# A mixture-of-experts kernel that stops zeroing its row buffer in stripes and loads rows with direct transfers on GpSimd

## The chip, the cores and the metric

One core of a Trainium2 chip runs the whole kernel as one program. The metric is the device time of a run in microseconds (us). The core has five engines that run side by side and meet only at semaphores: TensorE (PE, with its weight loads shown as PEld), VectorE (DVE), ScalarE (ACT), GpSimd (POOL) and SyncE (SP). Transfers issued by SP, ACT and POOL are carried out by the core's 16 DMA engines.

## The reference

Eight batches of 256 tokens with 128 channels go through three stages. Stage 1 and stage 3 are the same block: RMS norm, attention with rotary embedding, a window and a sink, projection, then a layer of 32 experts of which each token takes four. Stage 2 is another attention. Cut to what matters:

```
x = x + ffn_block(x) / 2          # stage 1: attention, then experts
x = x + mid_attention(layernorm(x))
x = x + ffn_block(x) / 2          # stage 3: same weights as stage 1

ffn_block: h  = x + attention(rmsnorm(x))
           g  = rmsnorm(h);  top4 experts of g @ gate_w + gate_b, softmax weights
           out = h + sum over the 4 of weight * (silu-gated up(g)) @ W_down
```

## The kernel before

The order of the program on each engine is `attention(layers[0])`, `experts(0)`, a barrier, `attention(layers[1])`, a barrier, `attention(layers[2])`, `experts(1)`. So five stretches follow each other: first attention, first experts, middle attention, last attention, last experts. The first and the last attention come from the same Python code and the same plan; they differ only where the code says `L is layers[0]`.

**Attention of a stage with experts.** Work is cut into frames; a frame makes scores of one group of heads for one tile of 128 tokens (PE, line 793), and side work (rotary projections, turning, projection, gate) is put between by a plan made in Python. In a rotary step DVE writes `rot_b` (line 1043, one of `RING` = 4 buffers), POOL adds it into `qT` or `keyT` with rows swapped by two accumulating transfers (`add_swapped`, line 1527), and DVE may write the same buffer of `rot_b` again only when those have landed. At a tile's end the reciprocal row sums make a round trip through DRAM: SP stores them (`turned<-rT`, line 622), loads them back spread over the partitions (`spread<-turned`, line 637), and POOL multiplies (`yT`, line 1628) before PE can project. SP also loads the expert weights during this stretch, in both stages.

**Routing.** After the gate, each tile's rows are scattered by POOL to `routed`, a DRAM buffer with a region of 2048 rows for each expert (`send`, line 1610, four indirect transfers of a tile). The row's place is expert times `REGION` plus the number of earlier rows of this expert.

**Zeroing.** An expert's rows are worked off in blocks of 128, counted from the start of its region, so its last block reads past its rows. All that a block may read must be finite. Therefore, in the first attention only, ACT issues sixteen transfers of 2 MB each (`blank_next`, line 1431), each of which zeroes one stripe of 128 rows in all 32 regions ahead of the tile whose rows could first reach it; POOL waits for a stripe (`blanked`) before it accounts for the tile.

**Experts.** DVE and PE make the plan: number of blocks of each expert, first row of each of the 96 blocks (`block_rows`, and `rows_at` with the partition added), and offset of its weights (`block_w`). Then 24 groups of four blocks are taken: rows are loaded into one of `XSLOTS` = 7 slots, two blocks by SP (line 688, direct, the row read into a register with line 683) and two by POOL (line 1709, indirect, with the rows' indices in `rows_at`); PE turns them (line 921), multiplies (931, 942, 950), and SP stores the answers. Answers are gathered by POOL later.

Of the kernel before, what the change touches and what calls it, by code (L numbers as in the profile page):

```python
# [42 lines left out]
REGION = TOKENS  # L43
# [4 lines left out]
XROWS = E * REGION + P  # L48
# [120 lines left out]
def primed(name):  # L169
# [11 lines left out]
    w_loaded=16 * E, count_full=1, nb_step=3, end_full=1, end_step=2, plan_full=1, plan_step=7,  # L181
# [139 lines left out]
def build(nc, x, table, masks, ffn_w, mid_w, columns, rows, w_up, w_down, out):  # L321
# [6 lines left out]
    with ExitStack() as ctx:  # L328
# [88 lines left out]
        earlier = sb("earlier", [P, E], BF16)  # L417
# [9 lines left out]
        nb_more = sb("nb_more", [E, TILES])  # L427
        nb_one = sb("nb_one", [E, 1])
        nb = sb("nb", [E, P], BF16)
        chosen = sb("chosen", [E, 2, NBLOCKS])  # L430
        block_row = sb("block_row", [P, NBLOCKS])
# [3 lines left out]
        rows_at = sb("rows_at", [P, NBLOCKS], U32)  # L435
# [20 lines left out]
        blanked = [sem(f"blanked{n}") for n in range(4)]  # L456
# [113 lines left out]
        def _(sp):  # L570
# [35 lines left out]
            def attention(L):  # L606

                if L.ffn:
                    if L is layers[0]:
                        sp.dma_start(routed[E * REGION:XROWS, :].rearrange("(p r) d -> p (r d)", p=P),  # L610
                                     nothing[:, 0:D]).then_inc(pads_zero, 16)
                S = L.signals

                def store_rows(k, lt):

                    tile, par = 4 * k + lt, lt % 2
                    turn = 2 * k + lt // 2
# [48 lines left out]
                body()  # L666

            def experts(number):
# [4 lines left out]
                sp.wait_ge(pads_zero, 16)  # L673
                sp.wait_ge(*S.at("plan_step", 7))
# [30 lines left out]
        def _(pe):  # L705
# [3 lines left out]
            def attention(L):  # L709
# [35 lines left out]
                def tail_step(k, misc, use, kind, arg):  # L745
# [21 lines left out]
                    elif kind == "place":  # L767
# [3 lines left out]
                        last = pe.matmul(misc[:, 0:E], mk[:, B_ONE:B_ONE + P], earlier[:, :], start=False, stop=True)  # L771
# [121 lines left out]
            def experts(number):  # L893
# [4 lines left out]
                pe.matmul(ps[0:E, BANK_XT, 0:NBLOCKS], earlier[:, :], mk[:, B_ONE:B_ONE + NBLOCKS],  # L898
# [4 lines left out]
                pe.matmul(ps[:, BANK_XT, 256:256 + E], nb[:, :], mk[0:E, B_BEFORE:B_BEFORE + E],  # L903
                          start=True, stop=True).then_inc(S["end_full"], 1)
                pe.wait_ge(*S.at("end_step", 2))
                pe.matmul(ps[:, BANK_Y, 0:2 * NBLOCKS], ones, chosen[:, :, :].rearrange("e a b -> e (a b)"),
                          start=True, stop=True).then_inc(S["plan_full"], 1)
                pe.wait_ge(*S.at("plan_step", 7))
# [69 lines left out]
        def _(dve):  # L978
# [24 lines left out]
            def attention(L):  # L1003
# [124 lines left out]
                def tail_step(k, misc, use, kind, arg):  # L1128
# [32 lines left out]
                    elif kind == "place":  # L1161
# [11 lines left out]
                        dve.tensor_copy(row_at[:, lt, :], place[:, :]).then_inc(S["place_step"], 1)  # L1173
# [63 lines left out]
            def experts(number):  # L1237
                S = moe[number]
                count = ps[0:E, BANK_XT, 0:NBLOCKS]
# [9 lines left out]
                dve.tensor_reduce(nb_one[:, :], nb_more[:, :], AX.X, ALU.add).then_inc(S["nb_step"], 1)  # L1249
                dve.wait_ge(*S.at("nb_step", 2))  # L1250
                dve.tensor_copy(nb[:, :], nb_one[:, 0:1].broadcast_to([E, P])).then_inc(S["nb_step"], 1)
                dve.wait_ge(*S.at("end_full", 1))
                dve.wait_ge(*S.at("nb_step", 3))
                dve.tensor_tensor(chosen[:, 0, :], block[0:E, :], end, ALU.is_ge).then_inc(S["end_step"], 1)
                dve.wait_ge(*S.at("end_step", 1))
                dve.tensor_tensor(chosen[:, 1, :], chosen[:, 0, :], nb[:, 0:NBLOCKS], ALU.mult)\
                    .then_inc(S["end_step"], 1)
                dve.scalar_tensor_tensor(first_at[:, :], ps[:, BANK_XT, 256:256 + E], float(P),
                                         tb[:, T_BASE:T_BASE + E], ALU.mult, ALU.subtract)\
                    .then_inc(S["plan_step"], 1)  # L1260
                dve.wait_ge(*S.at("plan_full", 1))
                dve.scalar_tensor_tensor(block_row[:, :], block, 0.0, plan[:, 1, :], ALU.add, ALU.subtract)\
# [3 lines left out]
                dve.wait_ge(*S.at("plan_step", 2))  # L1266
                dve.tensor_scalar(block_row[:, :], block_row[:, :], float(P), None, ALU.mult)\
                    .then_inc(S["plan_step"], 1)
                dve.wait_ge(*S.at("plan_step", 4))
                dve.scalar_tensor_tensor(region_row[:, :], plan[:, 0, :], float(REGION), block_row[:, :],  # L1270
                                         ALU.mult, ALU.add).then_inc(S["plan_step"], 1)
                dve.wait_ge(*S.at("plan_step", 5))
                dve.tensor_scalar(block_rows[:, :], region_row[:, :], float(E * REGION), None, ALU.min)\
                    .then_inc(S["plan_step"], 1)
                dve.tensor_scalar(rows_at[:, :], region_row[:, :], float(E * REGION), tb[:, T_PART:T_PART + 1],
                                  ALU.min, ALU.add).then_inc(S["plan_step"], 1)
# [69 lines left out]
        def _(act):  # L1346
# [9 lines left out]
            def attention(L):  # L1356
# [68 lines left out]
                def blank_next(k, lt):  # L1425

                    if k:
                        act.wait_ge(blanked[lt], 16 * k)
                    to = routed[0:E * REGION, :].rearrange("(e t r) d -> t e (r d)", e=E, t=TILES)
                    to = to[4 * k + lt:4 * k + lt + 1].rearrange("o e (c n) -> (o e) c n", n=BLANK)  # L1430
                    act.dma_start(to, nothing[0:E, :].unsqueeze(1).broadcast_to([E, STRIPE // BLANK, BLANK]))\
                        .then_inc(blanked[lt], 16)

                def body():
                    for frame in L.plan:
                        if L is layers[0]:
                            for k, lt in at_slot(frame, (2, 6, 10, 14)):
                                blank_next(k, lt)
# [61 lines left out]
        def _(pool):  # L1500
# [4 lines left out]
            def attention(L):  # L1505
# [89 lines left out]
                def account(k, lt):  # L1595
# [101 lines left out]
            def experts(number):  # L1697
# [72 lines left out]
```

## Time and profile before

| what | value |
|---|---|
| median of 3 runs | 1367.88 us (1364.82 to 1372.32) |
| profiled execution, device time | 1374.12 us |
| its span in the profile | 1372.3 us |
| busy in the span: PE, DVE, POOL, ACT | 1009.0, 806.2, 790.2, 570.7 us |
| mean granted TensorE clock | 0.879 of full speed |
| bytes moved by the transfers | 137.75 MB |
| `routed<-nothing` on ACT's queue | 16 issues of 2048 KB, 13.6 us to landing |

The busy times overlap and say nothing of which stretch waits for what; that has to be read from each stretch. "us to landing" is from the issue of a transfer to the semaphore that says it is in place.

### The profile page before, as it was taken

Reading aid. Unit: us, or ns where it says so; the run is one execution under the profiler, and the core shown is the slowest. Engines: PE = TensorE matmul, PEld = TensorE weight load, DVE = VectorE, ACT = ScalarE, POOL = GpSimd, SP = SyncE. Lnnn points to the kernel's source line nnn. Section 1 sums busy time; section 2 is a strip of 40 time slices with the busy share of each in tenths; the row PEclk is TensorE's granted clock in tenths of the full one; section 3 lists DMA queues with packets and bytes.
Section 4 is the critical chain, followed back from the end, with each engine's and each line's share of the span. In section 5 each row is a group of like instructions: output and inputs, shape, how many; then the busy total and the mean of one; then the engine's idle time right before and its main releaser. Section 6 shows DMA issues by size and latency. Waiting matters only on the chain.

```text
span 1372.3 us, 23277 instructions
## 1 busy us (share of the span) xinstructions
PE 1009.0 (74%) x6906; PEld 710.3 (52%) x6906; DVE 806.2 (59%) x2096; ACT 570.7 (42%) x2204; POOL 790.2 (58%) x1020
## 2 busy tenths in 40 slices
PE   2969788797735893599999947989888884689300
PEld 2646565564524773356666635656556553577200
DVE  4747777775531442378788637888888764143122
ACT  0535454454502441255565622655555461344100
POOL 3325587665577512657775314477877757751476
PEclk9889999998957997599999977999999996799755
DMA  7778999977613432011111103454543321343222
GB/s 181 144 166 178 197 206 202 192 159 163 142 51 102 133 101 62 21 36 32 36 41 32 24 16 62 105 124 90 129 99 84 66 55 49 109 134 99 69 63 59
DMA packets 121814, 137.75 MB, mean 100 GB/s; under 512 B 16864, under 2 KB 96992, under 8 KB 121696
## 3 DMA queue, kind: packets, MB, share of 16 engines
q1 hardware_dynamic: 86928, 57.99, 15.8%
q0 software_dynamic: 24064, 44.07, 15.2%
q10 hardware_dynamic: 10704, 34.21, 12.1%
q8 instruction: 62, 1.02, 0.3%
q14 instruction: 56, 0.46, 0.1%
HBM read 57.24 MB, written 58.07 MB: 84 GB/s over the span
## 4 chain that ended last, share of the span: by engine, by line
PE 38%; DVE 12%; POOL 9%; issue 7%; DMA 2%; ACT 1%; POOLq 1%; DVEq 0%; ACTq 0%
PE ps L931 6%; PE ps L820 5%; POOL shared L1719 4%; PE ps L838 4%; PE ps L950 4%; PE ps L733 3%; PE ps L855 3%; PE ps L793 3%; DVE top L1101 3%; PE ps L759 2%; DVE shift L1104 2%; PE ps L942 2%; PE ps L921 2%; DVE pT L1109 2%; DVE xr L1184 1%
## 5 line engine op out<-in xcount | busy, mean ns | idle before, releaser
L1373 ACT ACTIVATE prob<-ps,shift 128x128 f32<-128x128 f32 (+1 forms) x768 | 312.8, 422 | 165.0 <-DVE shift L1104 162.5
L1101 DVE TENSOR_REDUCE top<-ps 128x4 f32<-128x512 f32 (+1 forms) x192 | 182.7, 952 | 64.7 <-PE ps L793 32.2
L838 PE MATMUL ps<-tb,prob 128*128 128x128 f32 x1152 | 170.5, 285 | 1.5 <-DVE pT L1109 1.0
L1628 POOL TENSOR_TENSOR yT<-yraw,spread 128x1024 f32<-128x1024 f32 (+1 forms) x48 | 82.5, 1720 | 152.3 <-DMA spread<-turned 150.9
L838 PEld LDWEIGHTS ps<-tb,prob 128*128 128x128 f32 x1152 | 130.3, 144 | 70.5 <-issue 60.6
L1373 ACT ACTIVATION_READ_ACCUMULATOR prob<-ps,shift 128x1 f32 x768 | 158.7, 207 | 0.0
L1109 DVE COPY pT<-ps 128x512 f32<-128x512 f32 x192 | 131.4, 684 | 42.4 <-PE ps L838 42.2
L1610 POOL DMA_INDIRECT routed<-row_out,row_at x128 | 132.9, 1038 | 27.1 <-issue 26.6
L855 PE MATMUL ps<-pT,v 128*64 128x256 f32 x768 | 114.7, 405 | 23.3 <-issue 14.9
L1395 ACT ACTIVATE yraw<-ps 128x256 f32<-128x256 f32 x128 | 49.1, 383 | 184.6 <-PE ps L855 152.8
L793 PE MATMUL ps<-keyT,qT 64*128 64x256 f32 (+1 forms) x1024 | 125.5, 366 | 0.0
L1709 POOL DMA_INDIRECT qT<-routed,rows_at x96 | 90.7, 945 | 57.3 <-PE ps L921 29.3
L1527 POOL DMA_DIRECT2D qT<-rot_b x128 | 115.8, 1165 | 5.5 <-DVE qT L1043 5.2
L759 PE MATMUL ps<-wf,yT 128*128 128x128 f32 x512 | 76.0, 311 | 43.2 <-POOL yT L1628 40.7
L820 PE MATMUL ps<-shared,qT 128*128 128x256 f32 (+1 forms) x256 | 107.1, 519 | 0.5 <-ACT prob L1373 0.2
L793 PEld LDWEIGHTS ps<-keyT,qT 64*128 64x128 f32 x1024 | 81.8, 196 | 44.6 <-issue 37.8
L733 PE MATMUL ps<-xT,wf 128*128 128x256 f32 x320 | 93.4, 424 | 11.3 <-DVE pT L1109 5.8
L1291 DVE COPY prob<-ps 128x512 f32<-128x512 f32 x48 | 33.2, 692 | 115.8 <-PE ps L942 110.0
L1043 DVE SCALAR_TENSOR_TENSOR rot_b<-ps,bias_col,tb 128x256 f32<-128x256 f32 x160 | 69.5, 476 | 51.6 <-PE ps L733 30.7
L1719 POOL DMA_INDIRECT shared<-answers,answer_at x64 | 61.3, 957 | 60.2 <-DMA answers<-yraw 41.0
L759 PEld LDWEIGHTS ps<-wf,yT 128*128 128x128 f32 x512 | 71.8, 224 | 46.4 <-issue 44.4
L1634 POOL DMA_INDIRECT swapped<-answers,answer_at x64 | 62.4, 975 | 55.2 <-DMA answers<-yraw 41.4
(156 smaller groups left out, 1902.9 us busy)
## 6 DMA issues: line engine op xcount, KB each, us to landing
routed<-nothing ACTq DMA_DIRECT2D x16, 2048.0 KB, 13.6
qT<-rot_b POOLq DMA_DIRECT2D x128, 128.0 KB, 4.2
spread<-turned SPq DMA_DIRECT2D x64, 256.0 KB, 4.7
answers<-yraw SPq DMA_DIRECT2D x48, 256.0 KB, 2.3
shared<-in_w_up SPq DMA_DIRECT2D x32, 256.0 KB
qT<-routed SPq DMA_DIRECT2D x96, 64.0 KB, 2.0
keyT<-rot_b POOLq DMA_DIRECT2D x32, 128.0 KB, 3.2
shared<-in_w_down SPq DMA_DIRECT2D x32, 128.0 KB
```

The source lines that it names most:

```text
L733: last = pe.matmul(misc[:, n * T:(n + 1) * T], w[:, 0:P], xT[:, :], start=True, stop=True)
L759: last = pe.matmul(misc[:, 0:D], yT[:, n * P:(n + 1) * P], w, start=(n == 0), stop=(n == blocks - 1))
L793: last = pe.matmul(ps[:, bank + side, T * n:T * n + keys(lt)], qT[rows, j, 2 * g + n, q0:q0 + P], keyT[rows, j, g // 2, 0:keys(lt)], start ...
L820: last = pe.matmul(to, q, heads, start=behind, stop=not behind and n == 1)
L838: last = pe.transpose(ps[:, BANK_SIDE + bank, h * P:(h + 1) * P], prob[:, s % 4, h, c * P:(c + 1) * P], ident)
L855: last = pe.matmul(y[DH * side:DH * side + DH, 0:2 * P], v[:, j, c, at:at + DH], pT[:, s % 2, c, 2 * P * side:2 * P * side + 2 * P], start ...
L1101: dve.tensor_reduce(top1[:, s % 2, :], score_view(L, s, lt), AX.X, ALU.max, negate=True)\
L1109: dve.tensor_copy(pT[:, s % 2, 0, :], ps[:, BANK_SIDE + L.turned[k, s][0][0], :]).then_inc(S["pT_ready"], 1)
L1373: last = act.activation(prob[:, s % 4, h, 0:keys(lt)], score_view(L, s, lt)[:, h, :], ACT.Exp, bias=shift[:, lt % 2, one:one + 1], accum_o ...
L1527: pool.dma_start(to[n:P:2].rearrange("p n t -> p (n t)"), rot_b[1 - n:P:2, r % RING, :], accum_op=ALU.add).then_inc(S[f"swapped{r % RING}" ...
L1610: pool.indirect_dma_start(routed, bass.IndirectOffsetOnAxis(row_at[:, lt, n:n + 1], 0), row_out[:, lt, :], None).then_inc(S[f"sent{lt}"], 16)
L1719: pool.indirect_dma_start(last_answers[:, tile, n, :], None, answers, bass.IndirectOffsetOnAxis(answer_at[:, tile, n:n + 1], 0))\
```

## The change

The expert's blocks are counted from the end of its rows: its last block ends with its last row, and its first block may begin ahead of its first row. For that the rows of an expert start 128 rows into its region, and only these 128 rows ahead of each region are zeroed, once, by one SP transfer of 2 MB at the start. The sixteen stripe transfers and the waits for them go. Two more count matmuls, four more DVE instructions and fewer others make the plan. POOL reads the block's first row into a register and issues a direct transfer, as SP does, in place of the indirect one.

```
-REGION = TOKENS
+REGION = TOKENS + 4 * P
-XROWS = E * REGION + P
+XROWS = E * REGION + 2 * P
+NO_ROWS = E * REGION + P
...
-                        sp.dma_start(routed[E * REGION:XROWS, :].rearrange("(p r) d -> p (r d)", p=P),
+                        sp.dma_start(routed[NO_ROWS:XROWS, :].rearrange("(p r) d -> p (r d)", p=P),
                                      nothing[:, 0:D]).then_inc(pads_zero, 16)
+                        ahead = routed[0:E * REGION, :].rearrange("(e r) d -> e (r d)", e=E)[:, 0:STRIPE]
+                        sp.dma_start(ahead.rearrange("e (c n) -> e c n", n=BLANK),
+                                     nothing[0:E, :].unsqueeze(1).broadcast_to([E, STRIPE // BLANK, BLANK]))\
+                            .then_inc(pads_zero, 16)
...
-                dve.tensor_tensor(nb_more[:, :], count[:, 0:TILES], tb[0:E, T_IOTA16:T_IOTA16 + TILES], ALU.is_gt)\
+                dve.tensor_tensor(nb_more[:, :, :], count[:, :, 0:TILES],
+                                  tb[0:E, T_IOTA16:T_IOTA16 + TILES].unsqueeze(1).broadcast_to([E, 2, TILES]), ALU.is_gt)\
                     .then_inc(S["nb_step"], 1)
...
-                def blank_next(k, lt):
-
-                    if k:
-                        act.wait_ge(blanked[lt], 16 * k)
-                    to = routed[0:E * REGION, :].rearrange("(e t r) d -> t e (r d)", e=E, t=TILES)
-                    to = to[4 * k + lt:4 * k + lt + 1].rearrange("o e (c n) -> (o e) c n", n=BLANK)
-                    act.dma_start(to, nothing[0:E, :].unsqueeze(1).broadcast_to([E, STRIPE // BLANK, BLANK]))\
-                        .then_inc(blanked[lt], 16)
...
-                        if L is layers[0]:
-                            for k, lt in at_slot(frame, (2, 6, 10, 14)):
-                                blank_next(k, lt)
...
-                    if L is layers[0]:
-                        pool.wait_ge(blanked[lt], 16 * (k + 1))
-                    pool.tensor_tensor(earlier[:, :], earlier[:, :], picked[:, :], ALU.add).then_inc(S["picked"], 1)
+                    if L is layers[0] and tile == 0:
+                        pool.wait_ge(pads_zero, 32)
+                    pool.tensor_tensor(earlier[:, 0:E], earlier[:, 0:E], picked[:, :], ALU.add).then_inc(S["picked"], 1)
...
-                pool.wait_ge(pads_zero, 16)
-                pool.wait_ge(*S.at("plan_step", 7))
+                pool.wait_ge(pads_zero, 32)
+                pool.wait_ge(*S.at("plan_step", 3))
...
-                        pool.indirect_dma_start(
-                            rows_in[:, g % XSLOTS, b, :], None, routed,
-                            bass.IndirectOffsetOnAxis(rows_at[:, c:c + 1], 0)).then_inc(S[f"x_pooled{g % XSLOTS}"], 16)
+                        at = pool.value_load(block_rows[0:1, c:c + 1], min_val=0, max_val=XROWS - P)
+                        pool.dma_start(rows_in[:, g % XSLOTS, b, :], routed[bass.ds(at, P), :])\
+                            .then_inc(S[f"x_pooled{g % XSLOTS}"], 16)
```

The instruction order on ACT at the start of the first attention, before; `yraw`, `prob` and `sexp` are the attention's, `routed<-nothing` is a stripe of zeros:

```order
L1373 ACTIVATE prob,total<-ps,shift 128x128 x8
L1431 DMA routed<-nothing 32x16x1024
L1395 ACTIVATE yraw<-ps 128x256
L1373 ACTIVATE prob,total<-ps,shift 128x128 x4
L1395 ACTIVATE yraw<-ps 128x256
```

The same place in the changed kernel:

```order
L1388 ACTIVATE prob,total<-ps,shift 128x128 x8
L1410 ACTIVATE yraw<-ps 128x256
L1388 ACTIVATE prob,total<-ps,shift 128x128 x4
L1410 ACTIVATE yraw<-ps 128x256
L1388 ACTIVATE prob,total<-ps,shift 128x128 x4
```

All sixteen such rows are gone from ACT. SP's rows at the end of the initial loads in the changed kernel, where the one transfer of 32x16x1024 numbers now stands right behind the pads and ahead of the first store of row sums:

```order
L610 DMA routed<-nothing 128x128
L613 DMA routed<-nothing 32x16x1024
L626 DMA turned<-rT 16x128
L641 DMA spread<-turned 64x4x256 x2
L655 DMA shared<-in_w_up 128x2x256
```

POOL at the start of the first experts, before: the last rows of the last tile are sent, then 48 indirect loads follow each other.

```order
L1604 TENSOR_TENSOR earlier<-earlier,picked 128x32
L1605 COPY place_of<-place 128x4
L1610 DMA routed<-row_out,row_at 65664x128 x8
L1709 DMA qT<-routed,rows_at 128x128 x48
L1634 DMA swapped<-answers,answer_at 128x128 x8
```

And in the changed kernel, where each of the 48 loads is a register load, three register instructions (ISA) and a transfer:

```order
L1607 TENSOR_TENSOR earlier<-earlier,picked 128x32
L1608 COPY place_of<-place 128x4
L1613 DMA routed<-row_out,row_at 82176x128 x8
L1712 TENSOR_LOAD block_rows
L1712 ISA x2
L1713 ISA
L1713 DMA qT<-routed 128x128
L1712 TENSOR_LOAD block_rows
L1712 ISA x2
L1713 ISA
L1713 DMA qT<-routed 128x128
```

The loads keep their place on POOL; what stands between them is new.

## Rows read from the trace of the kernel before

The columns of the first group are: stretch, its length, busy us and instructions of PE, PEld, DVE, ACT and POOL, granted clock, DMA share, GB/s. A timeline row is: start, us, engine, line, what, and in brackets the idle time before it and what ended that.

**Rows 1.** Windows from first to last score, first and last attention

```profile
38.50:369.30 330.80, 270.92 (x1870) 183.88 (x1871) 228.43 (x602) 161.71 (x697) 196.46 (x281) 0.91 0.84 178
840.60:1128.20 287.60, 259.50 (x1872) 176.84 (x1871) 234.51 (x602) 163.71 (x698) 196.83 (x281) 0.97 0.41 92
```

**Rows 2.** Timeline, POOL: the last tile accounted, first and last attention

```profile
407.00 0.24 POOL L1604 TENSOR_TENSOR earlier<-earlier,picked 128x32 bf16<-128x32 bf16 x1 [1.02 <-DVE row_at L1173]
...
1160.52 0.24 POOL L1604 TENSOR_TENSOR earlier<-earlier,picked 128x32 bf16<-128x32 bf16 x1 [1.03 <-DVE row_at L1173]
```

**Rows 3.** Timeline, SP's queue: first tile's store in both, load back in the first

```profile
64.12 0.33 SPq L622 DMA_DIRECT2D turned<-rT  x1
73.58 3.23 SPq L637 DMA_DIRECT2D spread<-turned  x2
...
866.31 0.32 SPq L622 DMA_DIRECT2D turned<-rT  x1
```

**Rows 4.** Timeline, POOL: the first tile's multiplication, first and last attention

```profile
87.52 2.34 POOL L1628 TENSOR_TENSOR yT<-yraw,spread 128x1024 f32<-128x1024 f32 x1 [26.98 <-DMA spread<-turned]
...
872.70 2.36 POOL L1628 TENSOR_TENSOR yT<-yraw,spread 128x1024 f32<-128x1024 f32 x1 [9.99 <-DMA spread<-turned]
```

**Rows 5.** Waits (us, times, longest), 19 to 408 us, then 797 to 1161

```profile
POOL yT L1628 <- DMA spread<-turned: 112.4, 15, 27.0
...
POOL yT L1628 <- DMA spread<-turned: 38.5, 11, 10.0
```

**Rows 6.** Landing of `turned<-rT` (line 622), 60 to 408, then 860 to 1161

```profile
DMA to landing us min/median/max: 6.7/8.2/9.4
...
DMA to landing us min/median/max: 1.4/1.4/1.7
```

**Rows 7.** DMA queues: ACT's, packets, MB and share of 16 engines, 38 to 369

```profile
q10 hardware_dynamic: 8167, 32.47, 47.7%
```

**Rows 8.** Landing of the swaps (line 1527): at 27, 40 to 52, 220 to 410

```profile
DMA to landing us min/median/max: 3.5/3.6/3.6
...
DMA to landing us min/median/max: 12.1/12.1/12.1
...
DMA to landing us min/median/max: 2.7/7.9/12.2
```

**Rows 9.** Timeline before the first scores; at the end the last attention's rstd alone

```profile
23.61 2.02 POOL L1527 DMA_DIRECT2D keyT<-rot_b  x2 [6.80 <-DVE keyT L1043]
27.88 0.87 DVE L1043 SCALAR_TENSOR_TENSOR rot_b<-ps,bias_col,tb 128x256 f32<-128x256 f32 x2
31.27 2.46 POOL L1557 TENSOR_TENSOR rstd<-powers,minus_half 128x4 f32<-128x4 f32 x1
...
857.28 1.03 POOL L1557 TENSOR_TENSOR rstd<-powers,minus_half 128x4 f32<-128x4 f32 x1 [5.30 <-DVE powers L1020]
```

**Rows 10.** Timeline, start of the first experts

```profile
411.30 0.27 DVE L1275 TENSOR_SCALAR rows_at<-region_row,tb 128x96 uint32<-128x96 f32 x1
419.71 1.00 POOL L1709 DMA_INDIRECT qT<-routed,rows_at  x1 [2.27 <-issue]
420.50 14.34 SPq L688 DMA_DIRECT2D qT<-routed  x14
421.01 0.97 POOL L1709 DMA_INDIRECT qT<-routed,rows_at  x1 [0.30 <-issue]
426.12 1.09 PE L921 MATMUL ps<-tb,qT 128*128 128x128 f32 x4 [1.23 <-DMA qT<-routed,rows_at]
```

**Rows 11.** Lines 683 (SP) and 1527 (POOL): ns min/median/max

```profile
L683 SPq TENSOR_LOAD <-block_rows x96: 261/273/662, 418.9 to 1255.7; - x96
...
L1527 POOL DMA_DIRECT2D qT<-rot_b x128: 848/1178/2030, 25.2 to 1088.9; - x128
```

**Rows 12.** Chain of waits in the first experts, one step of two groups

```profile
485.33 1.73 PE ps L931 x8
...
489.60 1.73 PE ps L931 x8
```

More of the change, by code:

```diff
@@ L416, in build @@
         picked = sb("picked", [P, E], BF16)
-        earlier = sb("earlier", [P, E], BF16)
+        earlier = sb("earlier", [P, E + 1], BF16)
         ranks = sb("ranks", [P, TOPK, E])
@@ L425, in build @@
         answer = swapped[:, :, :].rearrange("p a b -> p (a b)").rearrange("p (s t k d) -> p s t k d", s=2, t=2, k=TOPK)
-        nb_more = sb("nb_more", [E, TILES])
-        nb_one = sb("nb_one", [E, 1])
+        nb_more = sb("nb_more", [E, 2, TILES])
+        nb_two = sb("nb_two", [E, 2])
+        short_by = sb("short_by", [E, 2])
+        step_of = sb("step_of", [E, 2])
         nb = sb("nb", [E, P], BF16)
         chosen = sb("chosen", [E, 2, NBLOCKS])
-        block_row = sb("block_row", [P, NBLOCKS])
         region_row = sb("region_row", [P, NBLOCKS])
@@ L455, in build @@
         tail_step = sem("tail_step")
-        blanked = [sem(f"blanked{n}") for n in range(4)]
         prep = sem("prep")
@@ L672, in experts @@
                     sp.wait_ge(*L.signals.at(f"sent{n}", BATCH * 32))
-                sp.wait_ge(pads_zero, 16)
-                sp.wait_ge(*S.at("plan_step", 7))
+                sp.wait_ge(pads_zero, 32)
+                sp.wait_ge(*S.at("plan_step", 3))
                 def store(g):
@@ L770, in tail_step @@
                         pe.matmul(misc[:, 0:E], mk[:, B_ONE:B_ONE + P], mk[:, B_BASE:B_BASE + E], start=False, stop=False)
-                        last = pe.matmul(misc[:, 0:E], mk[:, B_ONE:B_ONE + P], earlier[:, :], start=False, stop=True)
+                        last = pe.matmul(misc[:, 0:E], mk[:, B_ONE:B_ONE + P], earlier[:, 0:E], start=False, stop=True)
                     last.then_inc(S["misc_full"], 1)
@@ L897, in experts @@
                 pe.wait_ge(*layers[2 * number].signals.at("picked", TILES))
-                pe.matmul(ps[0:E, BANK_XT, 0:NBLOCKS], earlier[:, :], mk[:, B_ONE:B_ONE + NBLOCKS],
+                for n in range(2):
+                    pe.matmul(ps[0:E, BANK_XT, n * NBLOCKS:(n + 1) * NBLOCKS], earlier[:, n:n + E],
+                              mk[:, B_ONE:B_ONE + NBLOCKS], start=True, stop=True)
+                pe.matmul(ps[:, BANK_Y + 1, E:2 * E], mk[:, B_ONE:B_ONE + P], earlier[:, 0:E],
                           start=True, stop=True).then_inc(S["count_full"], 1)
@@ L902, in experts @@
                           start=True, stop=True)
-                pe.matmul(ps[:, BANK_XT, 256:256 + E], nb[:, :], mk[0:E, B_BEFORE:B_BEFORE + E],
+                pe.matmul(ps[:, BANK_Y + 1, 0:E], nb[:, :], mk[0:E, B_UPTO:B_UPTO + E],
                           start=True, stop=True).then_inc(S["end_full"], 1)
-                pe.wait_ge(*S.at("end_step", 2))
+                pe.wait_ge(*S.at("end_step", 3))
                 pe.matmul(ps[:, BANK_Y, 0:2 * NBLOCKS], ones, chosen[:, :, :].rearrange("e a b -> e (a b)"),
                           start=True, stop=True).then_inc(S["plan_full"], 1)
-                pe.wait_ge(*S.at("plan_step", 7))
+                pe.wait_ge(*S.at("plan_step", 5))
                 pe.wait_ge(*S.at("w_loaded", 16 * E))
@@ L1172, in tail_step @@
                             dve.wait_ge(*S.at(f"sent{lt}", 64 * k))
-                        dve.tensor_copy(row_at[:, lt, :], place[:, :]).then_inc(S["place_step"], 1)
+                        dve.tensor_scalar(row_at[:, lt, :], place[:, :], float(P), None, ALU.add).then_inc(S["place_step"], 1)
                 def combine(b, par):
@@ L1238, in experts @@
                 S = moe[number]
-                count = ps[0:E, BANK_XT, 0:NBLOCKS]
+                count = ps[0:E, BANK_XT, 0:2 * NBLOCKS].rearrange("e (n c) -> e n c", n=2)
                 end = ps[0:E, BANK_HT, 0:NBLOCKS]
@@ L1250, in experts @@
                 dve.wait_ge(*S.at("nb_step", 2))
-                dve.tensor_copy(nb[:, :], nb_one[:, 0:1].broadcast_to([E, P])).then_inc(S["nb_step"], 1)
+                dve.tensor_copy(nb[:, :], nb_two[:, 0:1].broadcast_to([E, P])).then_inc(S["nb_step"], 1)
+                dve.scalar_tensor_tensor(short_by[:, :], nb_two[:, :], float(-P),
+                                         count[:, :, 0:1].rearrange("e n c -> e (n c)"), ALU.mult, ALU.add)\
+                    .then_inc(S["nb_step"], 1)
@@ L1252, in experts @@
+                dve.wait_ge(*S.at("nb_step", 4))
+                dve.scalar_tensor_tensor(step_of[:, 0:1], short_by[:, 1:2], float(REGION), short_by[:, 0:1],
+                                         ALU.add, ALU.subtract).then_inc(S["nb_step"], 1)
+                dve.wait_ge(*S.at("nb_step", 5))
+                dve.scalar_tensor_tensor(step_of[:, 1:2], nb_two[:, 0:1], float(-P), step_of[:, 0:1],
+                                         ALU.mult, ALU.add).then_inc(S["nb_step"], 1)
                 dve.wait_ge(*S.at("end_full", 1))
-                dve.wait_ge(*S.at("nb_step", 3))
@@ L1254, in experts @@
                 dve.tensor_tensor(chosen[:, 0, :], block[0:E, :], end, ALU.is_ge).then_inc(S["end_step"], 1)
                 dve.wait_ge(*S.at("end_step", 1))
-                dve.tensor_tensor(chosen[:, 1, :], chosen[:, 0, :], nb[:, 0:NBLOCKS], ALU.mult)\
+                dve.wait_ge(*S.at("nb_step", 6))
+                dve.tensor_scalar(chosen[:, 1, :], chosen[:, 0, :], step_of[:, 1:2], None, ALU.mult)\
                     .then_inc(S["end_step"], 1)
-                dve.scalar_tensor_tensor(first_at[:, :], ps[:, BANK_XT, 256:256 + E], float(P),
-                                         tb[:, T_BASE:T_BASE + E], ALU.mult, ALU.subtract)\
-                    .then_inc(S["plan_step"], 1)
+                dve.wait_ge(*S.at("end_step", 2))
@@ L1261, in experts @@
+                dve.tensor_scalar(chosen[0:1, 1, :], chosen[0:1, 1, :], short_by[0:1, 0:1], float(P), ALU.add, ALU.add)\
+                    .then_inc(S["end_step"], 1)
                 dve.wait_ge(*S.at("plan_full", 1))
-                dve.scalar_tensor_tensor(block_row[:, :], block, 0.0, plan[:, 1, :], ALU.add, ALU.subtract)\
+                dve.scalar_tensor_tensor(region_row[:, :], block, float(P), plan[:, 1, :], ALU.mult, ALU.add)\
                     .then_inc(S["plan_step"], 1)
@@ L1265, in experts @@
                     .then_inc(S["plan_step"], 1)
-                dve.wait_ge(*S.at("plan_step", 2))
-                dve.tensor_scalar(block_row[:, :], block_row[:, :], float(P), None, ALU.mult)\
+                dve.wait_ge(*S.at("plan_step", 1))
+                dve.tensor_scalar(block_rows[:, :], region_row[:, :], float(NO_ROWS), None, ALU.min)\
+                    .then_inc(S["plan_step"], 1)
+                dve.scalar_tensor_tensor(first_at[:, :], ps[:, BANK_Y + 1, 0:E], float(P),
+                                         tb[:, T_BASE:T_BASE + E], ALU.mult, ALU.subtract)\
                     .then_inc(S["plan_step"], 1)
                 dve.wait_ge(*S.at("plan_step", 4))
[L1270 to L1273, printed above, removed]
+                dve.tensor_tensor(first_at[:, :], first_at[:, :], ps[:, BANK_Y + 1, E:2 * E], ALU.subtract)\
                     .then_inc(S["plan_step"], 1)
-                dve.tensor_scalar(rows_at[:, :], region_row[:, :], float(E * REGION), tb[:, T_PART:T_PART + 1],
-                                  ALU.min, ALU.add).then_inc(S["plan_step"], 1)
                 def gated(g):
```

5 lines of the change are left out of this document (2 added, 3 removed).

## The prediction

> **What bounds the kernel now.** I read the kernel stretch by stretch, because the share of busy time hides that the same code runs twice. The first and the last attention have the same instructions, so I cut each from its first score to its last [rows 1]: 330.8 us against 287.6 us, with nearly the same counts on each engine. DVE, ACT and POOL are busy for the same time in both to within 6 us, PE for 11 us more in the first. What differs is the DMA share, 0.84 against 0.41, and the granted clock, 0.91 against 0.97. The full stretch, from the first score to the accounting of the last tile, is 407.0 - 38.5 = 368.5 us in the first and 1160.5 - 840.6 = 319.9 us in the last [rows 1, 2]. The difference is **48.6 us**.
>
> Next the timeline, to find where it is lost. The two first scores stand 802.1 us apart. The first store of row sums still stands 802.2 us apart (64.12 and 866.31); the load back, which must wait for the store's landing, is issued 9.5 us after the store in the first [rows 3]; in the last the store has landed after 1.4 [rows 6]. The multiplication that needs it begins at 87.5 and at 872.7, only 785.2 us apart: 17 us are gone on the first tile [rows 4]. The end of the stretch is 753.5 us apart, so 31.6 us more go on the other tiles. The waits name the same place: POOL stands 112.4 us for `spread<-turned` in the first attention, 38.5 us in the last [rows 5], and the store lands in 8.2 us there, in 1.4 us here [rows 6]. So the first attention is bound by small transfers that queue among others; the last one is not.
>
> Which others? Both stretches load the weights and swap the rotary rows. Only the first has the stripes of zeros: their queue takes 47.7% of 16 engines over 331 us, which is 158 us or 9.9 us for each of the sixteen [rows 7]. That share of 0.48 is more than the whole difference of the DMA shares (0.43).
>
> **The change part by part.** *Stripes removed.* Sixteen transfers of 9.9 us leave the first attention, and with them the only thing that makes it unlike the last. ACT's sixteen issues go too, which cost nothing on the path since ACT waits elsewhere. I take the last attention as the measurement of the first without stripes: **-48.6 us**. The stretch behind starts with its end, as a chain, so the gain is kept to the end.
>
> *One transfer of 2 MB at the start.* It has the shape of a stripe, so about 9.9 us of all 16 engines, and it is issued behind the initial loads on SP's queue, before the first scores, where no stripe was. There it meets the first swaps. The key's swap is issued at 23.6 and about 24.4, and DVE writes the same buffer again for the fifth rotary step at 27.88, with no idle time before it: the 3.5 us that the swap takes to land there are just enough [rows 8, 9]. If it lands in L, DVE is late by 24.4 + L - 27.9. POOL then has some slack, since its `rstd` is handed over at 31.27 and stands queued behind the swaps until 33.7, of which it needs about 1.0 itself: 1.4 us [rows 9]. So the first scores come late by L - 4.9. Bounds for L: 3.6 without company, 12.1 beside the first stripe; the median of the later swaps beside stripes is 7.9 [rows 8]. The cost is 0 to 7.2 us; I take the 7.9, as the new transfer is only one and comes behind loads on its own queue: **+3.0 us**. All is landed long before the first store at 64.
>
> *POOL waits only once* for the two pad transfers, at the first tile, near 128 us: free. The removed waits for stripes were met when they came.
>
> *The plan* now has two more small matmuls and some four more dependent DVE steps, of about 0.2 us each: 1 us or little more. It ended at 411.6 while POOL's sending kept SP and POOL from the first load until 419.7 [rows 10]. It has 7 us of cover; without that cover it would be 1 us on the path of each experts stretch. Where `first_at` is computed later, its reader is four groups on. Nothing. The addition of 128 in DVE's last placing step takes the place of a copy of the same size. Nothing.
>
> *POOL's loads.* A load was an indirect transfer each 1.3 us (419.71, 421.01). The new one is a register load, three register instructions and a direct transfer. SP does exactly that, fourteen times in a row, in 14.34 / 14 = 1.02 us a load [rows 10], and its store `turned<-rT` shows what one issue costs there, 0.33 [rows 3]; so the register part is 0.7. On POOL a direct issue costs 0.85 to 1.18 us [rows 11]. If the two overlap completely the price p is about SP's 1.02; if they follow each other it is 0.7 + 1.18 = 1.9. The swaps show that POOL takes two direct issues in 2.0 us or less although each is listed with 1.2 [rows 9, 11], so its sequencer runs ahead; I take p = 1.3. What this touches is the second group: PE turned it at 426.12, waiting for POOL's fourth load [rows 10]. The first load starts about as before: SP's first stands at 420.5 behind two register parts of 0.7, POOL's would stand behind one, near 419.8. The fourth load comes 0.1 + 3 x (p - 1.27) later: -0.7 us at p = 1.02, +0.2 at 1.3, +2.0 at 1.9. Twice: -1.3 to +4.0, taken **+0.4 us**. From then on a group takes 4.27 us of PE [rows 12] and two loads take 2.6, up to 3.8, with seven slots ahead: covered.
>
> The rows show a register load on SP at 0.27 us in the median [rows 11]. The Trainium skill, page "DMA: Bandwidth & Descriptors", section "Latency and other measured facts", gives such a load a floor of about 600 ns, which speaks against this part. By it a load would be 0.33 us dearer and the sum 2 us higher, as an estimate; SP's row is below that floor.
>
> **Sum.** -48.6 + 3.0 + 0.4 = -45.2 us. Against the profiled execution, 1374.1 of which 1372.3 are span, this is 1328.9. That execution stood 6.2 us above the median of the runs; from the median of 1367.9 the same sum gives **1322.7 us**.
>
> **The rivals.**
> - *First attention recovers only in part* (chance 0.10). The transfer at the start could hold back swaps and initial loads more than one wait's worth, so that the first stretch stays 15 to 25 us slower than the last; for it speaks that 12.1 us of landing are seen with a single stripe about, against it that everything up to the first store is 802 us apart although the first stripes already ran there and swaps landed in 12.1 [rows 3, 8]. Time 1335 to 1345.
> - *POOL becomes the bound of the experts* (0.05). Its price would be that of a register load that waits for the engine to be empty, and a direct issue as slow as the longest seen, 2.03 us [rows 11]: p = 2.7. Then 48 loads take 130 us where 24 groups take 102.5, which is 27 us twice and gives 1322.7 + 54 = 1377 us, slower than before. It binds from p = 2.14 and eats the whole gain from p = 2.6. Against it: no direct issue that stood alone is above 1.2 us.
> - *The stripes are not the cause* (0.03). The zeros go and the first attention stays as it is, because its row sums wait for weights or for something left from the start: 1367.9 + 3.4 = 1371 us. Against it: the weights are loaded in the last attention too, where the store lands in 1.4 us.
> - *As forecast* (0.82): 48.6 recovered, less 0 to 7.2, and -1.3 to +4.0 for POOL: 1318 to 1331.
>
> **How the numbers follow.** The runs of before spread by some 4 us about their median, so the forecast's own range is 1314 to 1334. Taking in the near side of partial recovery, the range is 1314 to 1336. About 0.5%, 7 us, is what a measurement can tell from no change. Faster by more than that: 0.82 + 0.10 and little else, 0.93. Slower: the POOL rival's far part and half of the third, 0.04; within 0.5%: 0.03.
>
> **What the profile of the changed kernel would show.** Right: DMA share of the first attention near 0.4, `turned<-rT` landing in under 2 us there, and the stretch from first score to last accounting close to 320 us. The first score would stand near 41 to 42 instead of 38.5, behind a new wait of DVE's `rot_b` for the key's swap. In the experts, PE's second turning would come within 1 us of before, and POOL would wait for PE (a free slot) as it does now; a POOL without such waits and PE waiting for `qT<-routed` in the middle would show the second rival. Middle attention, last attention and the final gathers should keep their lengths. The forecast is wrong if the first attention's store still lands in 8 us, or if the first scores slip by far more than 7 us.

## The result and the profile after

The changed kernel takes 1326.14 us in the median of 4 runs (1324.25 to 1328.26), the kernel before 1367.3 beside it. The ratio is 0.9695 with a 95% interval of 0.9662 to 0.9728: 3.1% faster. The prediction was 1322.7 with a range of 1314 to 1336. All times and ratios here are of executions in the chip's faster state; one execution of e2, at 1396.49 us, was in the slower one and is left out.

The page of the changed kernel. The second and third lines are 40 slices of the span, in tenths of the 16 DMA engines and in GB/s; the last two are queues with packets, MB and share.

```profile
span 1322.6 us, 23709 instructions
...
DMA  8445454431134320111111123545542311442222
GB/s 219 73 101 121 95 119 113 89 69 53 53 97 135 109 70 20 27 37 43 33 35 29 21 44 69 117 95 132 124 96 60 76 50 46 133 128 88 71 65 60
...
q1 hardware_dynamic: 87456, 60.08, 17.0%
...
q10 hardware_dynamic: 2256, 0.66, 0.3%
```

Slices 2 to 10 are now in the range of slices 24 to 33, the last attention; the first slice has the initial loads and the zeros. ACT's queue has nothing left but the initial weights. The same cut as in [rows 1], from first score to last score, for the first and the last attention of the changed kernel (stretch, length, busy us of PE, PEld, DVE, ACT, POOL, granted clock, DMA share, GB/s):

```profile
44.20:328.40 284.20, 255.33 (x1856) 174.77 (x1871) 233.13 (x602) 162.97 (x698) 196.80 (x281) 0.98 0.41 93
792.40:1078.20 285.80, 258.23 (x1856) 176.42 (x1871) 232.67 (x602) 163.02 (x697) 196.20 (x280) 0.97 0.41 92
```

330.8 us have become 284.2, and the two attentions are now alike in every column. TensorE's granted clock went from 0.91 to 0.98 in this stretch, in which PE was busy for 0.82 of the time before (270.92 of 330.80 us) and for 0.90 now (255.33 of 284.20 us). PE's busy time fell by 15.6 us at nearly the same count of matmuls, so some of the 46.6 us came by way of a faster PE; no run separates that part from the shorter waits. The waits that answer to [rows 5], for the first attention (us, times, longest):

```profile
POOL yT L1631 <- DMA spread<-turned: 41.0, 12, 10.8
...
DVE rot_b L1050 <- DMA keyT<-rot_b: 7.0, 1, 7.0
```

POOL's wait for the row sums fell from 112.4 to 41.0 us. The kernel before had waits of the second kind too, five of them with 19.0 us in all, but later in the stretch:

```profile
DVE rot_b L1043 <- DMA keyT<-rot_b: 19.0, 5, 5.1
```

Those five are gone, and the one of 7.0 us is new, ahead of the first score. The timeline shows what it is: SP's transfer of zeros, POOL's swap of the key, DVE waiting for it, and POOL's `rstd` and the first scores behind.

```profile
19.24 0.43 SPq L613 DMA_DIRECT2D routed<-nothing  x1
...
23.37 2.00 POOL L1530 DMA_DIRECT2D keyT<-rot_b  x2 [6.79 <-DVE keyT L1050]
...
34.49 0.88 DVE L1050 SCALAR_TENSOR_TENSOR rot_b<-ps,bias_col,tb 128x256 f32<-128x256 f32 x2 [7.03 <-DMA keyT<-rot_b]
...
37.88 1.62 POOL L1560 TENSOR_TENSOR rstd<-powers,minus_half 128x4 f32<-128x4 f32 x1
...
44.22 1.23 PE L797 MATMUL ps<-keyT,qT 64*128 64x128 f32 x8
```

The key's second swap was issued at 24.2, and DVE's wait for it ended at 34.4, 10.2 us later, where the swaps of this place landed in 3.5 us before [rows 8]. The zeros needed 13.9 us to land, until 33.1, so the swap landed only about a microsecond behind them. The first score came at 44.2 instead of 38.5. And the start of the first experts, which answers to [rows 10]:

```profile
359.96 0.24 POOL L1607 TENSOR_TENSOR earlier<-earlier,picked 128x32 bf16<-128x32 bf16 x1 [1.02 <-DVE row_at L1180]
...
364.53 0.20 DVE L1284 TENSOR_SCALAR block_rows<-region_row 128x96 int32<-128x96 f32 x1
...
373.42 0.58 POOL L1713 DMA_DIRECT2D qT<-routed  x1 [3.04 <-issue]
373.46 16.60 SPq L692 DMA_DIRECT2D qT<-routed  x16
374.58 0.57 POOL L1713 DMA_DIRECT2D qT<-routed  x1 [0.58 <-issue]
...
379.04 1.09 PE L928 MATMUL ps<-tb,qT 128*128 128x128 f32 x4 [1.15 <-DMA qT<-routed]
```

From the last accounting it is 19.1 us to PE's second turning, as before (426.12 - 407.0). POOL's first load stands 0.8 us later than the indirect one stood, but the loads then follow each other every 1.15 us instead of 1.27 and land in 2.2 us instead of 2.6.

The whole by stretches, each from one mark to the next (profiled executions, 1372.3 and 1322.6 us of span):

| stretch | before | after | difference |
|---|---|---|---|
| start to first score | 38.5 | 44.2 | +5.7 |
| first attention, to last accounting | 368.5 | 315.7 | -52.8 |
| first experts, to the first gather of answers | 126.5 | 126.5 | 0.0 |
| middle attention, to the last attention's first score | 307.1 | 305.9 | -1.2 |
| last attention, to last accounting | 319.9 | 317.3 | -2.6 |
| last experts, to the first gather | 124.8 | 126.0 | +1.2 |
| gathers and end | 87.0 | 86.9 | -0.1 |

The last four rows have no change of any weight in them. Their scatter is the scatter of a stretch from run to run: the last attention, the same instructions in all, took between 314.0 and 323.1 us in the profiled executions of this study.

### The profile page after: what moved, and what is told of

Its sections match the earlier page's. It is cut to its first block, busy times and chain, and to the rows that moved or that the text cites. A ratio compares the mean times of both kernels' runs of the same rounds, so it can differ in the third digit from the quotient of the medians.

```text
span 1322.6 us, 23709 instructions
## 1 busy us (share of the span) xinstructions
PE 986.4 (75%) x6863; PEld 697.3 (53%) x6910; DVE 809.2 (61%) x2100; ACT 571.0 (43%) x2204; POOL 751.3 (57%) x1020
## 3 DMA queue, kind: packets, MB, share of 16 engines
q8 instruction: 62, 1.02, 0.3%
## 4 chain that ended last, share of the span: by engine, by line
PE 57%; DVE 15%; POOL 11%; issue 9%; DMA 4%; ACT 2%; POOLq 1%; SPq 0%; DVEq 0%; ACTq 0%
PE ps L842 8%; PE ps L938 7%; PE ps L859 7%; PE ps L797 6%; PE ps L737 6%; PE ps L824 5%; PE ps L763 4%; POOL shared L1722 4%; PE ps L957 4%; DVE top L1108 3%; POOL routed L1613 2%; DVE pT L1116 2%; DVE shift L1111 2%; PE ps L789 2%; PE ps L949 2%
## 5 line engine op out<-in xcount | busy, mean ns | idle before, releaser
L1713 POOL DMA_DIRECT2D qT<-routed x96 | 51.5, 536 | 99.0 <-issue 96.8
L797 PEld LDWEIGHTS ps<-keyT,qT 64*128 64x128 f32 x1024 | 81.0, 194 | 42.6 <-issue 38.5
L737 PE MATMUL ps<-xT,wf 128*128 128x256 f32 x320 | 89.1, 408 | 13.7 <-DVE pT L1116 5.8
L938 PE MATMUL ps<-shared,prob 128*128 x384 | 94.7, 391 | 0.0
L859 PEld LDWEIGHTS ps<-pT,v 128*64 128x64 f32 x768 | 47.7, 139 | 64.7 <-issue 46.9
```

The lines of the kernel that those rows point to most:

```text
L737: last = pe.matmul(misc[:, n * T:(n + 1) * T], w[:, 0:P], xT[:, :], start=True, stop=True)
L797: last = pe.matmul(ps[:, bank + side, T * n:T * n + keys(lt)], qT[rows, j, 2 * g + n, q0:q0 + P], keyT[rows, j, g // 2, 0:keys(lt)], start ...
L859: last = pe.matmul(y[DH * side:DH * side + DH, 0:2 * P], v[:, j, c, at:at + DH], pT[:, s % 2, c, 2 * P * side:2 * P * side + 2 * P], start ...
L938: last = pe.matmul(to, eT[:, g % 2, b, :], weights[:, bass.ds(at[b], 2 * DFF)], start=True, stop=True)
```

## The experiments

Each run below stands beside runs of the kernel before on the same chip. That kernel had a median of 1373.3 us on the chip of e1 to e4, 1371.1 on that of e5 and 1371.7 on that of e6 to e9, so only ratios are compared across chips. "Ratio" is always to the kernel before, with its 95% interval in brackets. The gap from a store of row sums to its load back, which waits for the store's landing, is read from SP's rows for all 16 tiles of the first attention.

**e1: all stripes, into a buffer that nothing uses.** ACT's issues and POOL's waits are put back, with another target:

```
+    spare = nc.dram_tensor("spare", (E * TOKENS, D), F32).ap()
...
+                    to = spare.rearrange("(e t r) d -> t e (r d)", e=E, t=TILES)
+                    to = to[4 * k + lt:4 * k + lt + 1].rearrange("o e (c n) -> (o e) c n", n=BLANK)
+                    act.dma_start(to, nothing[0:E, :].unsqueeze(1).broadcast_to([E, STRIPE // BLANK, BLANK]))\
+                        .then_inc(blanked[lt], 16)
...
+                            for k, lt in at_slot(frame, (2, 6, 10, 14)):
+                                blank_next(k, lt)
```

> The changed kernel with all sixteen 2 MB transfers of zeros put back at their old frames, but written to a buffer that nothing else touches; ACT's issues and POOL's waits for them are as in the kernel before. Queue theory (the small round trips of the first attention stand behind the stripes on the 16 DMA engines): the first attention takes 368 us from first score to last accounting again, against 316, the store of row sums lands in about 8 us, and the total is 1326 + 50 = about 1376. Rival, the stripes hurt because they write the same DRAM buffer that the scatter writes: less than 10 us of it comes back, 1326 to 1336.

Measured: 1376.99 us, ratio to before 1.0021 (0.9979 to 1.0063). Waits of the first attention in e1:

```profile
POOL yT L1647 <- DMA spread<-turned: 106.3, 15, 18.3
DVE rot_b L1052 <- DMA keyT<-rot_b: 29.2, 6, 6.8
```

The first attention took 365.7 us, and the landing of its store 8.1 us in the median. So putting the stripes back brings back the whole loss, in whatever buffer they end. The rival, that they cost because they write the same buffer as the scatter, is out. The second line has 29.2 us where the kernel before has 19.0; one of its six waits is that of the changed kernel at the start. The edit puts back ACT's issues and POOL's waits together with the traffic; e6 below has four times as many issues and costs half, so the issuing is not what costs.

**e2: the stripes at another place of the tile.**

```
-                            for k, lt in at_slot(frame, (2, 6, 10, 14)):
+                            for k, lt in at_slot(frame, (8, 12, 16, 20)):
```

> The same sixteen transfers to the unused buffer, each issued six frames later within its tile (frames 8, 12, 16, 20 in place of 2, 6, 10, 14), that is just after the load back of the row sums has been issued and some 14 us ahead of the next store. Collision theory (what costs is only that a stripe is in the queues when the store and the load back come): most of the loss is avoided, the store lands in under 4 us in the median, total 1330 to 1350. Bandwidth theory (the DMA engines are simply too full over the stretch, 0.84 busy): the same bytes cost the same, 1370 to 1380.

Measured: 1384.05 us, ratio 1.0112 (1.0048 to 1.0176). Both expectations failed in part. The store did land early (1.8 us in the median), as the collision theory had it, but nothing was gained; the time is a little above the 1370 to 1380 of the bandwidth theory. One tile of e2 in the timeline, SP's queue, ACT's queue, POOL:

```profile
109.43 0.33 SPq L628 DMA_DIRECT2D turned<-rT  x1
...
110.84 1.67 SPq L643 DMA_DIRECT2D spread<-turned  x2
111.25 0.31 ACTq L1448 DMA_DIRECT2D spare<-nothing  x1
...
124.80 2.34 POOL L1647 TENSOR_TENSOR yT<-yraw,spread 128x1024 f32<-128x1024 f32 x1 [13.71 <-DMA spread<-turned]
```

The store was back after 1.4 us. The load back is two transfers; they were issued at 110.84 and 111.5, and the stripe came between them, at 111.25. POOL had the row sums only at 124.8, 13.3 us after the second was issued, where the load back lands in some 4 us when no stripe is about. I had placed the stripes by frames of the plan and thought the load back would be done by then. Here the collision had only moved from one hop of the round trip to the other. The wait for row sums was 112.3 us, as in the kernel before. The run doesn't separate the theories, since its edit didn't keep the stripes clear of the round trip, as it was meant to.

**e3: only the stripes of the even tiles.** `blank_next` and POOL's wait stand under `if lt % 2 == 0`.

> Only the eight transfers of the even tiles, at their old frames, to the unused buffer. Collision theory: every tile whose round trip meets a stripe loses about 3 us, so half of e1's loss, total near 1350. Bandwidth theory (loss grows only when the engines are near full): the DMA share falls to some 0.6, and less than a quarter of e1's loss remains, 1326 to 1338.

Measured: 1364.16 us, ratio 0.9943 (0.9907 to 0.9979). Both expectations missed: 1364 is above the 1350 of the collision theory and far above the 1338 of the bandwidth theory. By the ratios (0.9943, 1.0021 for e1, and 0.9691 for the changed kernel in e7) the eight stripes cost some 34 us of e1's 45, well over half. The profiled execution, at 1357.06 the fastest of the seven, shows less: its first attention took 346.4 us, which is 28 us above some 318 without stripes, where e1 has 48. So half of the stripes cost more than half of the loss; why the second eight cost less is open. The loss does not vanish at a DMA share of 0.63:

```profile
44.20:372.00 327.80, 279.52 (x1934) 190.78 (x1935) 236.18 (x619) 167.65 (x716) 202.75 (x291) 0.93 0.63 134
```

The rows within the run speak for the collision theory. The stores of two tiles that follow each other, each with its load back:

```profile
84.78 0.33 SPq L628 DMA_DIRECT2D turned<-rT  x1
93.64 1.47 SPq L643 DMA_DIRECT2D spread<-turned  x2
110.56 0.33 SPq L628 DMA_DIRECT2D turned<-rT  x1
111.97 1.24 SPq L643 DMA_DIRECT2D spread<-turned  x2
```

The gap goes on like this: in seven of the 16 tiles, every second one, it is 8.4 to 10.4 us, in the others 1.4 to 1.8.

**e6: the same bytes in quarters.**

```
+                    act.dma_start(to[:, 4 * q:4 * q + 4, :], nothing[0:E, :].unsqueeze(1).broadcast_to([E, 4, BLANK]))\
+                        .then_inc(blanked[lt], 16)
...
+                            for k, n in at_slot(frame, range(2, 18)):
+                                blank_next(k, n // 4, n % 4)
```

> The changed kernel with the zeros of all sixteen stripes put back, to the unused buffer, but as 64 transfers of 512 KB, one a frame, in place of 16 of 2 MB, one in four frames. Same bytes, same descriptors. Theory, a small transfer waits for what is queued ahead of it (a 2 MB transfer holds it for up to 9 us): at most 512 KB stand ahead now, a hop waits up to 3 us, so the store lands in 3 to 4 us and about half of e1's loss of 50 us goes: some 20 to 25 us above the changed kernel. Bandwidth theory (0.84 of the DMA engines busy, whatever the size of the pieces): 45 to 55 us above it.

Measured: 1352.58 us, ratio 0.9867 (0.9824 to 0.9911), against 0.9691 for the changed kernel on the same chip (e7): 23 us above it, as expected. First attention with the quarters:

```profile
44.20:350.00 305.80, 261.40 (x1847) 179.74 (x1863) 227.29 (x602) 161.06 (x693) 196.70 (x281) 0.95 0.82 191
```

and two gaps on SP's queue:

```profile
161.71 0.33 SPq L628 DMA_DIRECT2D turned<-rT  x1
166.08 2.64 SPq L643 DMA_DIRECT2D spread<-turned  x2
187.48 0.34 SPq L628 DMA_DIRECT2D turned<-rT  x1
192.72 1.26 SPq L643 DMA_DIRECT2D spread<-turned  x2
```

The engines are nearly as full as before (0.82 against 0.84), all bytes are there, yet half of the loss is gone. These two gaps are 4.4 and 5.2 us; over the 16 tiles they are 1.8 to 5.2 with a median of 4.0, where e1 has 8.2 and the changed kernel 1.5. POOL's wait for the row sums is 87.9 us, between e1's 106.3 and the changed kernel's 41.0. So the loss is not set by the bytes or by the DMA share alone. The edit makes the pieces smaller and also spreads them over the frames, and the run doesn't tell these two apart; both mean that less stands ahead of a small transfer when it is issued. The half that stays was not taken further.

**e4, e7, e8: the one transfer of zeros, later.** e7 is the changed kernel again. e4 and e8 are one kernel, on two chips: the transfer leaves SP's start and is issued by ACT in the third frame.

```
-                        sp.dma_start(ahead.rearrange("e (c n) -> e c n", n=BLANK),
...
+                        if L is layers[0] and f == 2:
+                            ahead = routed[0:E * REGION, :].rearrange("(e r) d -> e (r d)", e=E)[:, 0:STRIPE]
+                            act.dma_start(ahead.rearrange("e (c n) -> e c n", n=BLANK),
```

> The changed kernel with its one 2 MB transfer of zeros issued by ACT in the third frame of the first attention (where the first stripe was, near 44 us) and not by SP behind the initial loads. Theory: the new 7.0 us wait of DVE's rot_b for the key's swap goes, the first score stands at 38.5 again, and as the transfer is done before the first store of row sums at 64 nothing else slips: total 1326.1 - 6 = about 1320. Rival: the transfer costs its time wherever it stands, by delaying the second batch's swaps or the first round trip: 1324 to 1328.

> The changed kernel once more, as the base of this call's chip: ratio to the kernel before near 0.9695, first score near 44.2 us with DVE waiting 7 us for the key's swap.

> The kernel of e4 again, with the one 2 MB transfer of zeros at the third frame, beside e7 on the same chip. In e4 the first score stood at 38.4 but the first attention ended only 1.9 us earlier than in the changed kernel. Theory that the rest was the spread of an unchanged stretch from run to run (314 to 323 us in the last attention of the runs so far): ratio 0.4% below that of e7. Rival, the transfer costs its 5 us at any place: ratio equal to e7's.

Measured: e4 1327.19 us, ratio 0.9663 (0.9612 to 0.9715); e7 1329.5, 0.9691 (0.9658 to 0.9723); e8 1321.06, 0.9633 (0.9597 to 0.967). e7 shows again what the changed kernel showed, the first score at 44.0 behind a wait of 6.9 us for the key's swap. In e8 there is no such wait:

```profile
38.67 1.23 PE L793 MATMUL ps<-keyT,qT 64*128 64x128 f32 x8
...
44.08 0.36 ACTq L1440 DMA_DIRECT2D routed<-nothing  x1
```

The first score is back at 38.7, and the last accounting stands at 355.8 against 364.2 in e7. The median is 8 us lower than e7's. 5.3 us of this are the earlier first score and can be pointed at; the remainder is within the scatter of the stretches. The transfer itself took 13.4 us to land and delayed no row sums: the store lands in 1.3 us in the median, 2.0 at most. So here its cost lay in its place. e4's median fell into the range of the rival expectation (1324 to 1328), which held the transfer to cost the same anywhere; but the ranges had been set from 1326.1, beside which the kernel before took 1367.3 and not 1373.3, and with a wide interval and a long first attention (319.7 us) e4 could not decide.

**e9: in four pieces, frames 2 to 5.** Same place, a quarter of the chunks, `[:, 4 * f - 8:4 * f - 4, :]`, at each frame.

> The zeros in four transfers of 512 KB, issued by ACT in frames 2 to 5 of the first attention. Theory that small transfers wait for what stands ahead: the swaps of the second batch lose 3 us at most and have that slack, so it is as fast as e8 or up to 2 us faster, 0.4 to 0.6% below e7. Rival, four issues disturb more than one: equal to e7.

Measured: 1320.94 us, ratio 0.9623 (0.9589 to 0.9658). Equal to e8 within the intervals. Both are faster than the changed kernel by 0.6 to 0.7%; where one transfer meets nobody, cutting it adds nothing that shows.

**e5: the kernel before with direct loads on POOL.**

```
-                        pool.indirect_dma_start(
-                            rows_in[:, g % XSLOTS, b, :], None, routed,
-                            bass.IndirectOffsetOnAxis(rows_at[:, c:c + 1], 0)).then_inc(S[f"x_pooled{g % XSLOTS}"], 16)
+                        at = pool.value_load(block_rows[0:1, c:c + 1], min_val=0, max_val=XROWS - P)
+                        pool.dma_start(rows_in[:, g % XSLOTS, b, :], routed[bass.ds(at, P), :])\
+                            .then_inc(S[f"x_pooled{g % XSLOTS}"], 16)
```

> The kernel before with nothing changed but POOL's row loads, which become a register load and a direct transfer as in the changed kernel (the indices for the indirect loads are still made by DVE). Theory that the loads are covered by PE: a load each 1.15 us in place of 1.27, POOL's first load 0.7 us later, the second turning of rows within 0.3 us of before, total 1367.3 with at most 1 us either way. Rival: the experts stretches are longer by 1 us each, as the last one of the changed kernel seems to be (126.0 against 124.8 us): 1369 to 1370.

Measured: 1372.09 us, ratio 1.0015 (0.9993 to 1.0037). The loads in e5 (ns min/median/max, then landing):

```profile
L1710 POOL DMA_DIRECT2D qT<-routed x96: 534/537/587, 412.4 to 1239.2; - x96
...
DMA to landing us min/median/max: 2.0/2.2/4.2
```

It is no gain, and if there is a loss it is at most 5 us. The first experts of e5 took 126.1 us and the last 125.5, by the marks of the table above (126.5 and 124.8 before), so the +1.2 us of the last experts can't be told from scatter.

## Why the prediction was right, and where its terms were off

- **Stripes removed, -48.6 us.** Right in mechanism, and right in size to within the scatter of one execution. The stretch itself became 52.8 us shorter in the profiles. To the last accounting they moved by 407.0 - 360.0 = 47.0 us, where the prediction has -48.6 + 3.0 = -45.6: that these two are so close is partly luck, since the terms were off by 4.2 and 2.7 us in opposite directions. The idea to take the last attention as the measure of the first held: they are now 315.7 and 317.3 us. But one execution gives such a term only roughly. e5 has the same two attentions as the kernel before, and there they took 360.7 and 321.2 us, a difference of 39.5 and not 48.6. The mean of the first attention with stripes (368.5 and 360.7) less the mean without (315.7 in the changed kernel, 320.2 in e7, 319.7, 317.1 and 318.4 in e4, e8 and e9) is 46 us; with the 5.7 of the next term that makes the 41 us which the medians show. e1 shows that the stripes are the cause and not the buffer, e3 that single stripes hold single stores back, e6 that the same bytes cost half when they come in smaller pieces, spread out.
- **The transfer at the start, +3.0 us.** The mechanism was right to the instruction: DVE's `rot_b` of the fifth rotary step waits for the key's swap. The size was too small. The term rested on a landing of 7.9 us; it was 10.2. The formula of the prediction, landing less 4.9, gives 5.3 for that, and 5.7 was measured, so it is the landing that was mis-sized. I had argued that the zeros stand behind SP's own loads and are only one; the row of 12.1 in [rows 8], a swap beside the first stripe, was the nearer one. e8 takes the term away entirely.
- **POOL's loads, +0.4 us.** The price was 1.15 us a load, below the 1.3 taken and inside the bounds of 1.02 and 1.9. The second turning did not move: the first load came 0.8 us later, the fourth lost 0.4 of that by the shorter steps, and the landing is 0.4 us shorter. The late first load and the shorter landing were not in the sum, so that the term came out near nothing is in part luck. e5 finds no effect beyond its interval. The register load takes 0.29 us in the median on POOL:

```profile
L1712 POOLq TENSOR_LOAD <-block_rows x96: 285/291/716, 371.9 to 1193.4; - x96
```

  The Trainium skill, page "DMA: Bandwidth & Descriptors", section "Latency and other measured facts", has a floor of about 600 ns for such a load. These rows are below it in the median; only the longest, 0.72 us, is above.
- **The plan, nothing.** It was done 4.8 us after the last accounting instead of 4.6, 7 us ahead of the first register load that reads it (371.9).
- **The total.** The profiled executions differ by 49.7 us, the medians by 41.2, the prediction by 45.2. The execution profiled of before was 6 us above its median, that of after 2 us below; the prediction named the first of these. The measured ratio's interval holds the predicted 0.967.
- **The rivals.** POOL as the bound did not come: PE has no wait for rows in the middle of the experts, and POOL still waits for free slots there. That the stripes are not the cause is refuted by the result and by e1. Recovery in part is what the transfer at the start did, but for 6 us, not for 15 to 25.

## What to carry to other kernels

When the same code runs twice in a program, once beside a background transfer and once without, the second run measures what the transfer costs; cut both at the same marks, and take more than one execution, since here one gave 48.6 us and another 39.5. A transfer that nothing on the critical path waits for can still set the time, if a short dependent round trip through memory has to pass the same DMA engines: first make it unnecessary, then put it where no round trip is due, and if neither can be had, cut it small and spread it. A bulk transfer at the start of a program should not be issued ahead of the first small transfers that gate the pipeline, only because its queue is idle by then.

## What was not expected of the hardware

- A small transfer beside a 2 MB one lost far more than half of its rate here: the key's swap landed 10.2 us after its issue and 1.3 us after the zeros did, against 3.5 us without them; the landing of the 8 KB store beside stripes is 8.2 us against 1.4; and in e2 a load back whose second half was issued just behind a stripe took 13.3 us. That it is held until the bulk is almost done is how I read these; no run shows the order within a DMA engine.
- A direct load of 128 rows keeps POOL busy for 0.53 us, where the swaps, also direct and with half as many rows of four times the length that are added to the target, take 0.85 and more [rows 11], and the indirect load took 0.94. Between two loads POOL shows 0.6 us without work, in which its register instructions stand, so I put the pace of 1.15 us down to these and the issue together; it is close to SP's 1.04 (16.60 us for 16 loads).
- An untouched attention stretch of some 318 us varies by 9 us from one execution to the next, more than several terms of the sum.
